# GpSimd's two-sided clamp with its operations swapped, and a new written order of steps on four engines

## The reference

```python
xn = (x - mean) / sqrt(var + 1e-5)                     # over the channels
shifted = xn moved down by one row, first row 0
k, v, r = (xn*m + shifted*(1-m)) @ W                    # a mix vector and a 128x128 weight each
# a scan over time, td = -exp(time_decay):
#   max_out = max(mx, k+tf); out = (e^(mx-max_out)*num + e^(k+tf-max_out)*v) / (e^(mx-max_out)*den + e^(k+tf-max_out))
#   max_st = max(mx+td, k);  num, den, mx = decayed by e^(mx+td-max_st) and fed with e^(k-max_st)
s = (sigmoid(r) * out) @ Wo
h = relu(xn @ w1 + b1) @ w2 + b2                        # 128 -> 512 -> 128, expert 0 alone counts
g = silu(layernorm(xn + h) * gamma + beta)
result = x + s * g
```

## Time and profile before

| | us |
|---|---|
| median of 3 runs | 134.46 (133.47 to 134.66) |
| the profiled execution, whole | 134.19 |
| its span, first to last instruction | 132.4 |
| busy in the span: PE, DVE, ACT, POOL | 108.0, 104.2, 99.8, 93.3 |
| mean granted TensorE clock | 0.955 |

### The profile page before, as it was taken

The page is one execution under the profiler, slowest core; times in us unless marked ns, Lnnn a source line. Parts: engine busy times, 40 slices in busy tenths (PEclk is TensorE's granted clock), DMA queues, the critical chain, the costliest instruction groups (busy, mean ns, idle before and its releaser), DMA issues. The chain is left out here.

```text
span 132.4 us, 1678 instructions
## 1 busy us (share of the span) xinstructions
PE 108.0 (82%) x340; PEld 57.8 (44%) x340; DVE 104.2 (79%) x208; ACT 99.8 (75%) x154; POOL 93.3 (70%) x124
## 2 busy tenths in 40 slices
...
GB/s 121 264 344 144 2 0 0 0 2 5 0 0 2 0 0 0 0 0 14 68 0 0 5 0 79 0 0 0 0 2 82 0 51 29 0 2 84 0 158 79
DMA packets 9450, 5.09 MB, mean 38 GB/s; under 512 B 480, under 2 KB 9184, under 8 KB 9440
## 3 DMA queue, kind: packets, MB, share of 16 engines
...
...
## 5 line engine op out<-in xcount | busy, mean ns | idle before, releaser
L620 PE MATMUL ps_z<-hid,w_c 128*128 128x512 f32 x64 | 30.8, 599 | 0.2 <-issue 0.2
L585 PE MATMUL ps_up<-xT_hi,w_hi 128*128 128x512 f32 x32 | 20.8, 651 | 7.2 <-POOL xT_hi L340 2.6
L445 ACT ACTIVATE hid<-ps_up,vec 128x512 f32<-128x512 f32 x32 | 21.1, 680 | 4.7 <-PE ps_up L587 4.6
L368 POOL TENSOR_SCALAR gap_max<-gap,td 128x512 f32<-128x512 f32 x8 | 16.6, 2072 | 1.7 <-DVE gap L745 1.2
L620 PEld LDWEIGHTS ps_z<-hid,w_c 128*128 128x128 f32 x64 | 11.4, 189 | 12.5 <-issue 9.5
L327 POOL TENSOR_SCALAR xn<-x_sb,neg_mean,rstd 128x128 f32<-128x128 f32 x28 | 15.0, 546 | 0.2 <-POOL rstd L313 0.2
L587 PE MATMUL ps_up<-xT_lo,w_hi 128*128 128x512 f32 x32 | 13.1, 409 | 0.0
L586 PE MATMUL ps_up<-xT_hi,w_lo 128*128 128x512 f32 x32 | 13.0, 406 | 0.0
L585 PEld LDWEIGHTS ps_up<-xT_hi,w_hi 128*128 128x128 f32 x32 | 6.5, 202 | 14.9 <-issue 9.5
L752 DVE TENSOR_TENSOR_SCAN den<-e_keep,e_new 128x512 f32<-128x512 f32 x8 | 10.5, 1312 | 2.4 <-ACT e_new L473 2.3
L376 POOL TENSOR_TENSOR dv<-v_sb 128x512 f32<-128x512 f32 x8 | 9.3, 1157 | 4.4 <-ACT v_sb L487 4.4
...
## 6 DMA issues: line engine op xcount, KB each, us to landing
...
```

Of the source, the lines that this page charges most:

```text
L368: pool.tensor_scalar(gap_max[n][:, :], gap[n][:, :], td[:, :], HIGHEST, ALU.max, ALU.min).then_inc(done["gap_max"], 1)
L445: act.activation(hid[b % 2][:, f, :], ps_up[f % 2][:, :], ACT.Relu, bias=vec[:, B1_COLUMN + f:B1_COLUMN + f + 1]).then_inc(done[f"hid{f}"], 1)
L585: pe.matmul(dst, hi, xT_hi[n][:, :], start=True, stop=False)
L620: ins = pe.matmul(ps_z[b % 2][:, :], w2_c[:, f, :], hid[b % 2][:, f, :], start=False, stop=last, skip_group_check=True)
```

## The change

1. `gap_max` becomes min with HIGHEST, then max with the column td: the same value.
2. All four lists of `PROGRAM` are reordered. Each holds the same steps as before (124 on PE, 154 on ACT, 144 on DVE, 86 on POOL).
3. Three waits of GpSimd are new or wider: for its own three constants at the start; `rstd1` of batch 1 also waits for `rstd1` of batch 0 (ScalarE's); `norm1` of batch 1 also waits for `T` of batch 0.

```diff
 PROGRAM = {
     "pe": """
-        T:0 b2m up0:0 up3:0 k:0 up2:0 up1:0 z3:0 z2:0 z0:0 T:1 z1:0 v:0 up1:1 var:0 up0:1 k:1 up3:1 r:0
+        b2m T:0 up1:0 up0:0 T:1 up3:0 k:0 up2:0 v:0 z0:0 z1:0 z3:0 z2:0 up1:1 up0:1 var:0 r:0 up3:1 k:1 z1:1
...
-        k:7 z0:6 back:3 r:5 up0:7 var:6 up3:7 v:6 s:4 r:6 back:4 z1:7 z3:7 up2:7 z0:7 v:7 z2:7 s:5 r:7 s:6
-        var.a:7 var.b:7 back:5 back:6 s.a:7 s.b:7 back.a:7 back.b:7
+        back:3 up2:7 k:7 r:5 z1:6 up3:7 v:6 z0:7 z2:7 z1:7 var:6 z3:7 s:4 v:7 var.a:7 back:4 r:6 s:5 back:5
+        r:7 s:6 var.b:7 back:6 s.a:7 s.b:7 back.a:7 back.b:7
     "act": """
-        ln_exp ve0 rs0 w1_hi neg_td xT:0 xT_hi:0 hid0:0 wo hid3:0 hid2:0 hid1:0 xT:1 e_keep:0 e_new:0 sq:0
+        ln_exp neg_td w1_hi ve0 rs0 xT_hi:0 xT:0 hid1:0 wo hid0:0 xT:1 hid2:0 hid3:0 e_new:0 e_keep:0 v_sb:0
...
-        e_new:3 rstd2:2 e_keep:3 ln_den:2 v_sb:2 hid2:3 xT:4 silu_set th_a:2 sq:3 th_g:2 silu:1 ln_exp
-        ln_var:3 hid0:4 rstd2:3 ln_den:3 hid1:4 silu_set th_r:2 hid2:4 xT:5 th_g:3 v_sb:3 hid3:4 th_a:3
-        silu:2 silu:3 th_r:3 sq:4 ln_exp ln_var:4 e_new:4 rstd2:4 hid0:5 v_sb:4 hid1:5 e_keep:4 xT:6 hid2:5
-        hid3:5 ln_den:4 silu_set th_g:4 th_a:4 ln_exp e_new:5 sq:5 e_keep:5 hid1:6 hid2:6 ln_var:5 e_new:6
+        silu_set silu:1 th_a:1 th_g:1 sq:2 hid1:3 th_r:1 hid0:3 ln_exp ln_var:2 rstd2:2 e_new:2 e_keep:2
+        hid2:3 hid3:3 xT:4 e_keep:3 ln_den:2 v_sb:2 sq:3 e_new:3 hid0:4 ln_var:3 rstd2:3 hid3:4 silu_set
+        th_g:2 th_r:2 th_a:2 xT:5 hid1:4 silu:2 hid2:4 ln_exp ln_den:3 e_keep:4 sq:4 e_new:4 hid0:5 v_sb:3
+        ln_var:4 ln_den:4 rstd2:4 hid1:5 silu_set th_g:3 xT:6 hid2:5 th_r:3 hid3:5 th_a:3 silu:3 th_g:4
...
-        th_a:5 sq:6 th_g:6 th_a:6 th_r:5 ln_exp ln_var:6 e_keep:7 v_sb:6 e_new:7 hid0:7 hid3:7 rstd2:6
-        ln_den:7 silu_set th_r:6 hid2:7 th_g:7 v_sb:7 silu:5 silu:6 th_a:7 sq.a:7 sq.b:7 th_r:7 ln_exp
-        ln_var.a:7 ln_var.b:7 rstd2.a:7 rstd2.b:7 silu_set silu.a:7 silu.b:7
+        silu_set th_g:6 hid2:7 th_r:5 v_sb:6 th_a:6 sq:6 hid3:7 ln_exp ln_var:6 e_keep:7 sq.a:7 e_new:7
+        rstd2:6 v_sb:7 ln_var.a:7 ln_den:7 silu_set th_r:6 th_g:7 sq.b:7 th_a:7 silu:6 th_r:7 ln_exp
+        ln_var.b:7 rstd2.a:7 rstd2.b:7 silu_set silu.a:7 silu.b:7
     "dve": """
-        bnA:0 bnB:0 aggr1:0 norm1:0 bn:1 aggr1:1 one_minus cols xT_lo:0 w2_sum ink:0 bn:2 inr:0 aggr1:2
-        inv:0 mx:0 gap:0 bn:3 bn:4 aggr1:3 bn:5 xT_lo:1 den:0 ink:1 rel:0 inr:1 mx:1 zn:0 inv:1 aggr1:4
+        bnA:0 bnB:0 aggr1:0 bn:1 aggr1:1 norm1:0 w2_sum cols one_minus xT_lo:0 bn:2 ink:0 aggr1:2 inr:0
+        inv:0 mx:0 gap:0 ink:1 bn:3 aggr1:3 xT_lo:1 inv:1 bn:4 den:0 bn:5 inr:1 rel:0 zn:0 mx:1 gap:1 dev:0
...
-        ink:7 prod:3 dev:5 gated:4 mx:7 res:3 adev:5 gap:7 wkv:5 gated:5 inv:7 inr:7 prod:4 den:7 dev:6
-        adev:6 wkv:6 rel:7 res:4 zn:6 gated:6 prod:5 dev:7 prod:6 adev:7 wkv:7 res:5 gated:7 res:6 zn.a:7
+        gated:4 inv:7 den:6 dev:5 adev:5 rel:6 wkv:5 res:3 inr:7 mx:7 gap:7 dev:6 adev:6 gated:5 wkv:6
+        prod:4 den:7 res:4 zn:6 rel:7 prod:5 gated:6 res:5 dev:7 adev:7 prod:6 wkv:7 gated:7 zn.a:7 res:6
         zn.b:7 prod.a:7 prod.b:7 res.a:7 res.b:7
     "pool": """
-        w1_lo neg_mean1:1 Bk:0 Br:0 Bv:0 w2_c rstd1:1 norm1:1 gap_min:0 gap_max:0 xT_hi:1 neg_mean1:2 Bk:1
+        w1_lo rstd1:1 neg_mean1:1 norm1:1 Bk:0 Br:0 Bv:0 w2_c Bk:1 Bv:1 xT_hi:1 gap_min:0 gap_max:0 rstd1:2
...
-        keep:6 gap_max:7 gap_min:7 dv:6 keep:7 dv:7
+        keep:6 dv:6 gap_min:7 gap_max:7 dv:7 keep:7
...
             pool.memset(averager[:, :], 1.0 / H).then_inc(prep["consts"], 1)
+            pool.wait_ge(prep["consts"], 3)
...
                 after_rows(pool, b - 2)
+                if b == 1:
+                    after(pool, "rstd1", 0)
...
-                after(pool, "T", b - 2)
+                after(pool, "T", max(b - 2, 0))
...
-                pool.tensor_scalar(gap_max[n][:, :], gap[n][:, :], td[:, :], HIGHEST, ALU.max,
-                                   ALU.min).then_inc(done["gap_max"], 1)
+                pool.tensor_scalar(gap_max[n][:, :], gap[n][:, :], HIGHEST, td[:, :], ALU.min,
+                                   ALU.max).then_inc(done["gap_max"], 1)
```

More of the change, by code:

```diff
@@ L32 @@
-        k:7 z0:6 back:3 r:5 up0:7 var:6 up3:7 v:6 s:4 r:6 back:4 z1:7 z3:7 up2:7 z0:7 v:7 z2:7 s:5 r:7 s:6
-        var.a:7 var.b:7 back:5 back:6 s.a:7 s.b:7 back.a:7 back.b:7
+        b2m T:0 up1:0 up0:0 T:1 up3:0 k:0 up2:0 v:0 z0:0 z1:0 z3:0 z2:0 up1:1 up0:1 var:0 r:0 up3:1 k:1 z1:1
+        T:2 up2:1 z3:1 z0:1 z2:1 up1:2 up0:2 var:1 up3:2 v:1 s:0 k:2 T:3 up2:2 z3:2 z0:2 z2:2 r:1 z1:2 up1:3
+        up0:3 k:3 var:2 z1:3 up3:3 z0:3 up2:3 back:0 T:4 v:2 z2:3 z3:3 up0:4 var:3 up3:4 k:4 r:2 up2:4 up1:4
@@ L34 @@
+        T:5 s:1 z0:4 z3:4 z1:4 z2:4 back:1 up0:5 v:3 var:4 up2:5 up1:5 k:5 r:3 T:6 s:2 up3:5 z0:5 back:2
+        z2:5 z1:5 z3:5 k:6 up0:6 up1:6 var:5 v:4 up3:6 r:4 up2:6 s:3 T:7 z0:6 z2:6 v:5 up0:7 up1:7 z3:6
+        back:3 up2:7 k:7 r:5 z1:6 up3:7 v:6 z0:7 z2:7 z1:7 var:6 z3:7 s:4 v:7 var.a:7 back:4 r:6 s:5 back:5
+        r:7 s:6 var.b:7 back:6 s.a:7 s.b:7 back.a:7 back.b:7
     """,
     "act": """
-        ln_exp ve0 rs0 w1_hi neg_td xT:0 xT_hi:0 hid0:0 wo hid3:0 hid2:0 hid1:0 xT:1 e_keep:0 e_new:0 sq:0
@@ L37 @@
-        v_sb:0 hid1:1 ln_den:0 ln_var:0 hid0:1 rstd2:0 silu_set th_g:0 th_a:0 xT:2 hid3:1 hid2:1 th_r:0
-        ln_exp e_keep:1 sq:1 hid0:2 e_new:1 hid1:2 ln_var:1 v_sb:1 rstd2:1 ln_den:1 hid2:2 hid3:2 xT:3
-        silu_set th_r:1 th_g:1 silu:0 th_a:1 sq:2 ln_exp e_keep:2 hid1:3 hid0:3 e_new:2 ln_var:2 hid3:3
-        e_new:3 rstd2:2 e_keep:3 ln_den:2 v_sb:2 hid2:3 xT:4 silu_set th_a:2 sq:3 th_g:2 silu:1 ln_exp
-        ln_var:3 hid0:4 rstd2:3 ln_den:3 hid1:4 silu_set th_r:2 hid2:4 xT:5 th_g:3 v_sb:3 hid3:4 th_a:3
@@ L42 @@
-        silu:2 silu:3 th_r:3 sq:4 ln_exp ln_var:4 e_new:4 rstd2:4 hid0:5 v_sb:4 hid1:5 e_keep:4 xT:6 hid2:5
-        hid3:5 ln_den:4 silu_set th_g:4 th_a:4 ln_exp e_new:5 sq:5 e_keep:5 hid1:6 hid2:6 ln_var:5 e_new:6
-        rstd2:5 e_keep:6 v_sb:5 ln_den:5 hid3:6 xT:7 ln_den:6 silu_set th_g:5 hid0:6 silu:4 th_r:4 hid1:7
-        th_a:5 sq:6 th_g:6 th_a:6 th_r:5 ln_exp ln_var:6 e_keep:7 v_sb:6 e_new:7 hid0:7 hid3:7 rstd2:6
-        ln_den:7 silu_set th_r:6 hid2:7 th_g:7 v_sb:7 silu:5 silu:6 th_a:7 sq.a:7 sq.b:7 th_r:7 ln_exp
@@ L47 @@
-        ln_var.a:7 ln_var.b:7 rstd2.a:7 rstd2.b:7 silu_set silu.a:7 silu.b:7
+        ln_exp neg_td w1_hi ve0 rs0 xT_hi:0 xT:0 hid1:0 wo hid0:0 xT:1 hid2:0 hid3:0 e_new:0 e_keep:0 v_sb:0
+        sq:0 hid1:1 hid0:1 ln_var:0 ln_den:0 rstd2:0 hid3:1 silu_set th_g:0 xT:2 hid2:1 th_a:0 silu:0 th_r:0
+        sq:1 hid1:2 ln_exp ln_var:1 e_new:1 rstd2:1 e_keep:1 hid0:2 hid3:2 xT:3 ln_den:1 hid2:2 v_sb:1
+        silu_set silu:1 th_a:1 th_g:1 sq:2 hid1:3 th_r:1 hid0:3 ln_exp ln_var:2 rstd2:2 e_new:2 e_keep:2
@@ new lines @@
+        hid2:3 hid3:3 xT:4 e_keep:3 ln_den:2 v_sb:2 sq:3 e_new:3 hid0:4 ln_var:3 rstd2:3 hid3:4 silu_set
+        th_g:2 th_r:2 th_a:2 xT:5 hid1:4 silu:2 hid2:4 ln_exp ln_den:3 e_keep:4 sq:4 e_new:4 hid0:5 v_sb:3
+        ln_var:4 ln_den:4 rstd2:4 hid1:5 silu_set th_g:3 xT:6 hid2:5 th_r:3 hid3:5 th_a:3 silu:3 th_g:4
+        th_a:4 ln_exp e_keep:5 sq:5 e_new:5 hid0:6 hid1:6 ln_var:5 v_sb:4 rstd2:5 ln_den:5 hid3:6 e_keep:6
+        hid2:6 e_new:6 xT:7 silu_set th_r:4 th_g:5 th_a:5 silu:4 hid0:7 v_sb:5 silu:5 ln_exp ln_den:6 hid1:7
@@ L52 @@
[L52 to L56, removed]
@@ L57 @@
-        ink:7 prod:3 dev:5 gated:4 mx:7 res:3 adev:5 gap:7 wkv:5 gated:5 inv:7 inr:7 prod:4 den:7 dev:6
-        adev:6 wkv:6 rel:7 res:4 zn:6 gated:6 prod:5 dev:7 prod:6 adev:7 wkv:7 res:5 gated:7 res:6 zn.a:7
+        bnA:0 bnB:0 aggr1:0 bn:1 aggr1:1 norm1:0 w2_sum cols one_minus xT_lo:0 bn:2 ink:0 aggr1:2 inr:0
+        inv:0 mx:0 gap:0 ink:1 bn:3 aggr1:3 xT_lo:1 inv:1 bn:4 den:0 bn:5 inr:1 rel:0 zn:0 mx:1 gap:1 dev:0
+        xT_lo:2 adev:0 inv:2 aggr1:4 wkv:0 gated:0 bn:6 ink:2 inr:2 zn:1 den:1 mx:2 prod:0 aggr1:5 xT_lo:3
@@ new lines @@
+        rel:1 gap:2 inv:3 ink:3 inr:3 dev:1 mx:3 adev:1 gap:3 wkv:1 zn:2 den:2 res:0 aggr1:6 xT_lo:4 rel:2
+        inv:4 gated:1 ink:4 den:3 zn:3 mx:4 bn:7 inr:4 gap:4 dev:2 aggr1:7 prod:1 adev:2 xT_lo:5 ink:5 wkv:2
+        res:1 rel:3 den:4 gated:2 inv:5 rel:4 zn:4 mx:5 inr:5 prod:2 ink:6 xT_lo:6 res:2 gap:5 dev:3 adev:3
+        wkv:3 mx:6 gap:6 den:5 gated:3 inv:6 zn:5 inr:6 dev:4 adev:4 wkv:4 rel:5 xT_lo:7 prod:3 ink:7
+        gated:4 inv:7 den:6 dev:5 adev:5 rel:6 wkv:5 res:3 inr:7 mx:7 gap:7 dev:6 adev:6 gated:5 wkv:6
```

10 lines of the change are left out of this document (5 added, 5 removed).

## The result

| | before | after |
|---|---|---|
| median of the runs, us | 134.56 | 123.78 (123.38 to 123.84) |
| ratio, 95% interval | | 0.920 (0.913 to 0.927) |
| profiled execution, its span | 134.19, 132.4 | 123.78, 122.0 |
| start of gap:7, from there to the end | 108.28, 24.1 | 101.01, 21.0 |

The forecast was 128.8 us with a range of 125.0 to 133.2. The direction was right and the gain was nearly twice what was forecast, 10.8 instead of 5.7 us, outside the range.

The account below looks back on a forecast made before the run. POOL was taken to bound the front part. gap:7 at 108.28 + 0.4 + 1.9 - 4.9 = 105.7, plus an end of 21.0, 1.8 outside the span and 0.3 to the median, gave 128.8 us, range 125.0 to 133.2.

Parts of the forecast that it names:

- What bounds the kernel: Front part, 12.0 us to gap:7: POOL is the fullest engine, 83.00 of 96.28 us, and slow gap_max delays DVE.
- The price of the form: gap_max on POOL: the new form takes 0.68 us like gap_min, or at the other end stays at 2.00.
- I take two thirds, 4.9 us: Front part: of 7.3 us saved on the path 4.9 come through, since PE and DVE close up.
- The list: DVE's waits behind gap_max before den:1, zn:2, mixed_k:6 and zn:5: 1.3, 2.1, 2.6 and 1.3 us, sum 7.3.
- +0.4 for the start: Start: batch 0's normalisation comes 3.0 us later but mostly hidden, so gap:0 at 16.3 instead of 15.85 us.
- +1.9 for the three moved steps: DVE's wkv:5, inv:7 and inr:7 move from the end to before gap:7, lengthening the front by 1.9 us.
- The end: From gap:7 to the end of the span: 21.0 us instead of 24.12.
- The walk: Steps followed from gap:7 on: first silu half at 14.7, then 5.3 us as before, 20.0 us in all.
- The allowance of 1.0 us: Added to the end's 20.0 us for waits that such a walk misses.
- Rival one: Quick gap_max loses 0.9 of its 1.32 us to meetings with VectorE's reads: 132.4 us, chance 0.15.
- the pair at 50.98 and 51.66: Old kernel: gap_max took its 2.00 us though den overlapped it, both undisturbed; read as the slow form perhaps hiding meetings.
- Rival three: New order makes ScalarE stand before th_g:3, e_keep:3 and e_new:7, 3.0 us each: 137.8 us, chance 0.08.

Follow-up runs that it names:

- e5: Old kernel and order, quick form of gap_max (min, then max) for batches 4 and 5 alone: ratio 0.968.
- e6: Old kernel and order, quick form of gap_max for all batches but 4 and 5: 127.68 us, ratio 0.950.
- e12: Old kernel and order, quick form of gap_max for batch 1 alone: 132.17 us in one run.
- e1: Old kernel and order of steps, quick form of gap_max for all batches: 125.90 us, ratio 0.939.
- e4: Old kernel with four extra GpSimd instructions at the start, min and max in either order, column first or second: (max, min) 2.0 us, (min, max) 0.7.
- e7: New kernel with 19 instead of 11 warming matmul calls on TensorE: 122.48 us, ratio 0.913.
- e2: New kernel and order of steps with the old, slow form of gap_max: 133.11 us, ratio 0.991.

## Why the prediction was wrong, point by point

**What bounds the kernel.** Right. POOL was the fullest in the front, and gap_max was on DVE's path in the places read from the order. e5 and e6 show this for batches 4 and 5, e12 for batch 1, and e1 for all together.

**The price of the form.** Right at 0.68 against 0.69 us, and the likelier of two ends (e4).

**The step that failed: "I take two thirds, 4.9 us".** The list gave 7.3 us for the path, and I cut it because at 90% busy PE and DVE would close up. In e1 the operation alone brought gap:7 8.0 us forward: all of the list, and more. Its places measured 2.2, 2.5, 2.6 and 0.4 us where the list had 1.3, 2.1, 2.6 and 1.3; another 0.3 lay before gap:1. That the list's sum comes so near is partly luck, since the 0.9 missing at its first place (the wait before zn:1, behind TensorE's clock) and the 0.9 too much at its last cancel. Two things were wrong in the cut. DVE was in fact 79.06 of 88.27 us, 90% busy, in e1, and is 92% busy in the new kernel: 90% was no bar at all. And PE's busy time wasn't fixed work: 81.79 us of it in the old front became 78.51 in e1, as the clock of 0.97 became 1.00 and its matmuls ran shorter. I had counted slow matmuls as work that would stand in the way, when they were a result of the waits.

**The new order in the front.** I had it at +0.4 for the start and +1.9 for the three moved steps. Against e1 gap:7 is 0.7 us later: gap:0 is 2.6 later, and from gap:0 to gap:7 it takes 82.5 instead of 84.4 us although it holds the 1.9 us more work. So the order saves 3.8 us there, for which the prediction had no term; DVE's idle time in that stretch falls from 8.9 to 4.9 us. Which of the moved steps does it wasn't tested. The +0.4 missed the clock, 1.4 us (e7), and 0.8 us more, of which 0.5 is mixed_v, which DVE began at 14.88 behind the statistics of batch 2 and two other mixes, and not at 14.4.

**The end.** Forecast 21.0 us, measured 20.99. The walk itself was 1.0 us short: e_keep:7 started 3.45 us after gap:7 where I had 2.8, e_new:7 ended at 5.15 where I had 4.4, and the last pair of silu began at 15.7 where I had 14.7. I had POOL's two steps ready at 2.05; gap_min:7 took 1.53 and gap_max:7 1.10 us, and they were ready at 3.42. The allowance of 1.0 us, for which no row stood, was just what was missing, and the last part, 5.29 us here, took 4.86 in e6 and 5.81 in e1. The mechanism held; the hit to the tenth is luck.

**The sum.** 105.7 forecast for gap:7, 101.0 measured. Of the 4.7 us, 3.1 are the operation (8.0 for 4.9) and 1.6 the order (+0.7 for +2.3). With the whole 7.3 us of the list the forecast would have been 126.4 us, inside its range but still 2.6 too high. Outside the span 1.8 us, as said.

**Rival one** had the right mechanism and no weight. Three of eight quick maxima lost 0.4 to 1.0 us, and each lost it where the slow form loses it too in the same order of steps. The same three instructions in e2, one of which is

```profile
46.67 2.97 POOL L371 TENSOR_SCALAR gap_max<-gap,td 128x512 f32<-128x512 f32 x1
```

take 2.97, 2.79 and 2.41 us against 2.00, that is 0.97, 0.79 and 0.41 more; the quick ones took 1.66, 1.46 and 1.10 against 0.69, the same. So the slow form isn't immune, as the pair at 50.98 and 51.66 had made me think. In these three meetings DVE's instruction began before the maximum or within 0.02 us of it. The excess agrees in the main with the Trainium skill (SBUF — State Buffer, Who interferes with whom), by which the later of the two stands until the other is through: gap_max at 44.67 us lost 0.97 us while the scan dev, begun at the same time, ran for 1.26. In such a meeting the forms don't differ. Where the scan clearly begins second they may: in the old kernel den ran undisturbed inside a slow maximum twice (51.66 and 93.82, 1.22 and 1.25 us), against the rule, and in the new one a den that began at 50.07, inside the quick maximum at 49.90, took 1.60. One such case of 0.4 us proves nothing, and no run separates it. All told the meetings brought the eight maxima to a mean of 0.96 instead of 0.69 us.

**Rival three** didn't come: ScalarE stood under 0.5 us before th_g:3, e_keep:3 and e_new:7. With the slow form it begins to: in e2 ScalarE waits 2.16 us for gap_max before e_keep:3. The order fits the quick operation.
